# Expert outputs accumulated into stored rows, and every stage given a new place

## What is computed

```python
xn = layernorm(x)
x = x + cosformer(xn) + moe0(xn)      # linear attention, 16 heads; 2 shared experts + top 4 of 16
xn = layernorm(x)
x = x + softmax_attn(xn) + moe1(xn)   # causal, rotary, 16 heads of 8; one expert of 8 per token

# moe1, the last part: each token belongs to the expert with its greatest probability
route = softmax(xn @ router_w + router_b)
e, p = argmax(route), max(route)
a, g = split(xn @ w1[e])              # 128 -> 2 x 512
out = (silu(a) * g) @ w2[e] * p       # 512 -> 128, times that probability
```

## Time and profile before

| what | before |
|---|---|
| device time, median of 3 runs | 1369.88 us (1368.84 to 1372.6) |
| profiled execution: span, first to last instruction | 1371.5 us |
| profiled execution: own time | not given apart from the span; the 3 runs lie on both sides of it |
| PE busy | 1209.3 us, 88% of the span |
| DVE, ACT, POOL busy | 991.5, 912.8, 692.6 us |
| last matmul of the run starts | 1336.68 us |
| output DMAs | 4 of 1024 KB, 7.9 us to landing |
| granted TensorE clock, mean | 0.959 |

### The profile page before, as it was taken

How to read it: one execution, slowest core, us unless ns; L and a number is a source line. 1 busy time by engine, 2 the same in 40 slices (tenths; PEclk the granted TensorE clock), 3 DMA queues, 4 the chain that set the end, 5 groups by cost and what they waited for, 6 DMA issues and landing times.

```text
span 1371.5 us, 28942 instructions
## 1 busy us (share of the span) xinstructions
PE 1209.3 (88%) x10216; PEld 700.1 (51%) x10216; DVE 991.5 (72%) x2378; ACT 912.8 (67%) x1233; POOL 692.6 (50%) x1093
## 2 busy tenths in 40 slices
PE   2675999999999999999999999999986999899990
PEld 1342445445454545454454545454432476799990
DVE  2163888888888988888888989888868462344545
ACT  1141777778687868777786877787773667577760
POOL 6324455554536464554545464655543345466760
PEclk9898999999999999999999999999996799999995
DMA  7323505050524416060515335060615210111118
GB/s 224 63 57 64 111 19 115 20 103 27 96 53 71 91 32 120 11 115 20 103 34 88 72 52 105 19 120 14 111 37 171 74 29 25 31 48 50 50 48 250
DMA packets 80300, 100.90 MB, mean 74 GB/s; under 512 B 8800, under 2 KB 56672, under 8 KB 79776
## 3 DMA queue, kind: packets, MB, share of 16 engines
q1 hardware_dynamic: 75680, 89.85, 29.9%
q0 software_dynamic: 4480, 9.22, 2.3%
HBM read 73.50 MB, written 25.01 MB: 72 GB/s over the span
## 4 chain that ended last, share of the span: by engine, by line
PE 63%; DVE 20%; issue 5%; ACT 4%; POOL 4%; DMA 3%; ACTq 0%; SPq 0%; DVEq 0%; POOLq 0%
PE PS L628 9%; PE PS L595 8%; PE PS L440 7%; PE PS L484 7%; PE PS L561 5%; PE PS L639 4%; PE PS L580 4%; PE PS L423 4%; DVE xn L824 3%; PE PS L434 2%; DVE nm L985 2%; DMA early<-gate_rows 2%; PE PS L462 2%; PE PS L570 2%; DVE ra L933 1%
## 5 line engine op out<-in xcount | busy, mean ns | idle before, releaser
L735 ACT ACTIVATE flow<-PS 128x1024 f32<-128x1024 f32 x320 | 321.2, 1028 | 129.4 <-PE PS L580 112.1
L1146 POOL TENSOR_SCALAR_AFFINE_SELECT flow<-flow 128x256 f32<-128x256 f32 (+1 forms) x448 | 191.0, 444 | 374.3 <-ACT flow L735 371.7
L595 PE MATMUL PS<-flow 128*32 128x512 f32 (+3 forms) x2048 | 181.2, 455 | 6.2 <-POOL flow L1146 6.2
L985 DVE TENSOR_REDUCE nm<-PS 128x2 f32<-128x1024 f32 x128 | 154.6, 1220 | 42.3 <-PE PS L549 38.9
L1133 POOL TENSOR_TENSOR early<-early 128x512 f32<-128x512 f32 x128 | 160.7, 1270 | 20.9 <-DMA early<-gate_rows 20.0
L484 PE MATMUL PS<-early,down 128*128 128x512 f32 x288 | 151.8, 637 | 18.4 <-POOL early L1133 17.9
L726 ACT COPY qp<-PS 2x1024 f16<-2x1024 f16 x128 | 128.5, 1004 | 51.0 <-PE PS L570 49.8
L440 PE MATMUL PS<-xnT,up 128*128 128x512 f32 x288 | 152.6, 625 | 3.7 <-DVE at L908 3.4
L987 DVE TENSOR_REDUCE nm<-PS 128x2 f32<-128x768 f32 x128 | 121.6, 950 | 32.4 <-PE PS L549 32.3
L628 PE MATMUL PS<-xsT,w1s 128*128 128x128 f32 x1152 | 141.5, 276 | 3.0 <-DVE act L1079 2.9
L1076 DVE SCALAR_TENSOR_TENSOR tanh<-tanh,PS 128x512 f32<-128x512 f32 x72 | 49.5, 687 | 130.0 <-ACT tanh L769 130.0
(11 more groups left out here) (178 smaller groups left out, 2263.3 us busy)
## 6 DMA issues: line engine op xcount, KB each, us to landing
early<-gate_rows SPq DMA_DIRECT2D x32, 1024.0 KB, 10.8
qp<-relay_q SPq DMA_DIRECT2D x64, 128.0 KB
kp<-relay_k SPq DMA_DIRECT2D x64, 128.0 KB
xsb<-xs SPq DMA_DIRECT2D x76, 64.5 KB, 1.8
relay_k<-qkh SPq DMA_DIRECT2D x32, 128.0 KB, 2.3
early<-in_w SPq DMA_DIRECT2D x1, 4096.0 KB, 14.8
out_y<-X SPq DMA_DIRECT2D x4, 1024.0 KB, 7.9
relay_q<-qkh SPq DMA_DIRECT2D x16, 128.0 KB, 2.3
```

The costliest lines, as they stand in the source:

```text
L595: ins = pe.matmul(m.PS[32 * j:32 * j + 32, m.PV, kt * P:], m.vst[b % 2][:, kt, 4 * g + j, :], m.pt[:, r, k * L + o:k * L + o + L - kt * P] ...
L735: act.activation(m.pt[:, n % RING, :], m.PS[:, i:i + 2, :].rearrange("p k c -> p (k c)"), ACT.Exp, scale=1.0 / SCALE).then_inc(s["exp"], 1)
L985: dve.tensor_reduce(nm[:, 3, 2 * n:2 * n + 2], ps, AX_X, ALU.max, negate=True).then_inc(s["max"], 1)
L1146: ins = pool.affine_select(part, part, [[0, part.shape[1]], [1, P]], ALU.is_ge, nothing, base=0, channel_multiplier=-1)
```

## The change

Two things are changed together.

**The outputs of the second experts.** `ys` and its end are gone. `store` writes each batch's 512 rows of `X` to the output as soon as its attention is added (256 KB each, SP). ScalarE multiplies a tile's output by the token's probability while it copies it out of PSUM, and puts it into `X` itself, whose 64 tiles serve as the buffers. `scatter` (POOL) is an indirect DMA with `compute_op=ALU.add`: it adds the 128 rows onto the rows in the output tensor. The probability travels with the row in `xs`, whose rows are now 130 wide; blank rows carry a spare destination (2048 extra rows at the end of the output tensor, cut off afterwards) and probability 0, written from constants by 18 pad DMAs instead of 9. The destination is now one VectorE copy (`rows`) instead of three GpSimd operations. The first scatter waits for all 16 stores. `load` has 12 buffers and waits for the output copy of the tile 12 before it; the tile list has 72 entries instead of 76.

**The places.** All numbers of the tables are new, and each stage of each of the 72 tiles has its own number; from tile 31 on they are again 1.3 apart. 22 instead of 21 tiles use the shared banks.

```diff
 NTILE = B * NT + E1
 RING = 4
 SL = 5
-U = 4
-NTAB = NTILE + U
+U = 12
+NPAD = 2 * E1
+FIRSTS = B * NT - 2 * NT
+ROW = D + 2
+NTAB = NTILE
...
 FIRST = placed(
-    stats0=[-57.35],
-    norm0=[-49.85],
...
+    stats0=[-58.08],
+    norm0=[-51.44],
...
+    q=[-45.19],
+    kv=[-41.49],
...
 ATTENTION = placed(
-    score=[0, 0.1, 1.45, 3.05, 7.4, 8.2, 9.25, 10.3, 12.35, 13.05, 13.85, 14.05, 14.6, 14.7, 15.2, 15.35, 15.75,
...
-    mparts=[-2.85, 3.3, 8.15, 10.35],
-    mrows=[-0.85, 5.2, 10.4, 12.1],
...
+    max=[-9.06, -8.97, -8.72, -3.65, -2.28, -2.01, 0.93, 0.98, 1.36, 3.14, 4.03, 4.58, 4.76, 4.87, 5.22, 5.84, 6.37,
+         8.49, 10.01, 10.22],
+    mparts=[-2.14, 3.93, 5.97, 10.4],
+    mrows=[-0.98, 6.02, 10.06, 11.08],
...
+    out=[24.82],
+    store=[25.4])
...
 
     def outputs(_, n):
         act.wait_ge(s["yo_mm"], n + 1)
-        act.wait_ge(s[f"d_ys{n % U}"], 16 * (n // U + 1))
-        act.copy(m.ysb[:, n % U, :], wk(("outputs", 0, n))[:, 0:D]).then_inc(s["ycopy"], 1)
+        if n == 0:
+            act.wait_ge(s["d_out"], 16 * (B - 2))
+        if n == FIRSTS:
+            act.wait_ge(s["d_last"], 16 * 2)
+        if n == B * NT:
+            act.wait_ge(s["d_head"], 16 * E1)
+        act.activation(m.X[:, n % (B * NT), :], wk(("outputs", 0, n))[:, 0:D], ACT.Copy,
+                       scale=m.xsb[:, n % U, D + 1:D + 2]).then_inc(s["ycopy"], 1)
...
-        then(dve.tensor_reduce(m.pmax[:, b * NT:(b + 1) * NT], m.p1[:, :, :], AX_X, ALU.max))
+        then(dve.tensor_reduce(m.xn[1][:, :, D + 1], m.p1[:, :, :], AX_X, ALU.max))
...
+    def rows(_, n):
+        u = n % U
+        dve.wait_ge(s[f"d_xs{u}"], 16 * (n // U + 1))
+        dve.tensor_copy(m.rowu[:, n:n + 1], m.xsb[:, u, D:D + 1]).then_inc(s["rows"], 1)
...
-    n = B * NT // Q
-    for q in range(Q):
-        y, xq = m.yg[:, q * n:(q + 1) * n, :], m.X[:, q * n:(q + 1) * n, :]
-        dve.wait_ge(s[f"d_xs{q}"], 16 * (NTILE // U + 2))
-        then(dve.tensor_tensor(y, y, m.pmax[:, q * n:(q + 1) * n].unsqueeze(2).to_broadcast([P, n, D]), ALU.mult))
-        dve.tensor_tensor(xq, xq, y, ALU.add).then_inc(s["final"], 1)
```

```diff
-LAST = [(-19.5, "w1", 0), (-4.5, "w2", 0), (-13, "spares", 0)] + [(-12.4 + 1.2 * k, "tables", k) for k in range(6)]
...
+LAST = placed(
+    w1=[-27.19],
+    w2=[-11.16],
+    tables=[-14.1, -12.56, -10.07, -6.93, -6.76, -6.28],
+    pads=[-19.91],
...
+NBETWEEN = 22
```

```diff
-    def rows(_, n):
-        u = n % U
-        pool.wait_ge(s[f"d_xs{u}"], 16 * (n // U + 1))
-        pool.wait_ge(s[f"d_ys{u}"], 16 * (n // U + 1))
-        if n:
-            pool.wait_ge(s["nextspare"], n)
-        pool.tensor_scalar(m.isno[:, :], m.xsb[:, u, D:D + 1], 0.0, m.spare[:, 0:1], ALU.is_lt,
-                           ALU.mult).then_inc(s["spare"], 1)
-        pool.wait_ge(s["spare"], n + 2)
-        pool.tensor_scalar(m.rowu[:, u:u + 1], m.isno[:, :], m.xsb[:, u, D:D + 1], None, ALU.add).then_inc(s["rows"], 1)
-        pool.tensor_scalar(m.spare[:, :], m.spare[:, :], float(P), None, ALU.add).then_inc(s["nextspare"], 1)
-
-    def outputs(_, n):
-        u = n % U
+    def scatter(_, n):
+        if n == 0:
+            pool.wait_ge(s["d_out"], 16 * (B - 2))
+            pool.wait_ge(s["d_last"], 16 * 2)
+            pool.wait_ge(s["d_spare"], 16)
         pool.wait_ge(s["ycopy"], n + 1)
         pool.wait_ge(s["rows"], n + 1)
         alone()
-        pool.indirect_dma_start(m.ys_d, bass.IndirectOffsetOnAxis(ap=m.rowu[:, u:u + 1], axis=0),
-                                m.ysb[:, u, :], None).then_inc(s[f"d_ys{u}"], 16)
-
-    share = dict(stats0=stats0, stats1=stats1, q=q, gated=gated, score=scores, rope=rope, sort=sort, spares=spares, rows=rows,
-                 outputs=outputs)
+        pool.indirect_dma_start(m.rows_d, bass.IndirectOffsetOnAxis(ap=m.rowu[:, n:n + 1], axis=0),
+                                m.X[:, n % (B * NT), :], None,
+                                compute_op=ALU.add).then_inc(s["d_head" if n < E1 else "d_added"], 16)
...
         sp.wait_ge(s["rowzero"], 1)
+        marks = const(m, K_SP).rearrange("p (j c) -> p j c", c=2)
         for e in range(E1):
             row = sp.value_load(m.ti[0:1, 0, e:e + 1], min_val=0, max_val=E1 * CAP - P)
-            sp.dma_start(m.xs_d[bass.ds(row, P), :], m.zeros[:, :]).then_inc(s["d_pad"], 16)
-        sp.dma_start(m.xs_d[E1 * CAP:E1 * CAP + P, :], m.zeros[:, :]).then_inc(s["d_pad"], 16)
+            sp.dma_start(m.xs_d[bass.ds(row, P), 0:D], m.zeros[:, 0:D]).then_inc(s["d_pad"], 16)
+            sp.dma_start(m.xs_d[bass.ds(row, P), D:], marks[:, e, :]).then_inc(s["d_pad"], 16)
+        last = m.xs_d[E1 * CAP:E1 * CAP + E1 * P, :].rearrange("(j p) c -> p j c", p=P)
+        sp.dma_start(last[:, :, 0:D], m.zeros[:, 0:D].unsqueeze(1).to_broadcast([P, E1, D])).then_inc(s["d_pad"], 16)
+        sp.dma_start(last[:, :, D:], marks[:, E1:, :]).then_inc(s["d_pad"], 16)
...
             sp.wait_ge(s["rows"], n - U + 1)
-        row = sp.value_load(m.ji[0:1, 2, n:n + 1], min_val=0, max_val=E1 * CAP)
+            sp.wait_ge(s["ycopy"], n - U + 1)
+        row = sp.value_load(m.ji[0:1, 2, n:n + 1], min_val=0, max_val=E1 * CAP + (E1 - 1) * P)
         sp.dma_start(m.xsb[:, u, :], m.xs_d[bass.ds(row, P), :]).then_inc(s[f"d_xs{u}"], 16)
 
-    share = dict(gT=gT, parts=parts, relay=relayed, w1=w1, w2=w2, pads=pads, load=load)
+    def store(b, i):
+        if b == 0:
+            sp.dma_start(m.spare_d, m.zeros[:, 0:D].unsqueeze(1).to_broadcast([P, NPAD, D])).then_inc(s["d_spare"], 16)
+        sp.wait_ge(s["x2"], b + 1)
+        sp.dma_start(m.out_d[:, b], m.X[:, b * NT:(b + 1) * NT, :]).then_inc(s["d_out" if b < B - 2 else "d_last"], 16)
...
-    n = B * NT // Q
-    for u in range(U):
-        sp.wait_ge(s[f"d_ys{u}"], 16 * (NTILE // U + 1))
-    for q in range(Q):
-        src = m.ys_d[q * n * P:(q + 1) * n * P, :].rearrange("(t p) d -> p t d", p=P)
-        sp.dma_start(m.yg[:, q * n:(q + 1) * n, :], src).then_inc(s[f"d_xs{q}"], 16)
-    for q in range(Q):
-        sp.wait_ge(s["final"], q + 1)
-        sp.dma_start(m.out_d[:, q * B // Q:(q + 1) * B // Q].rearrange("p b t d -> p (b t) d"),
-                     m.X[:, q * n:(q + 1) * n, :]).then_inc(s["d_out"], 16)
-    sp.wait_ge(s["d_out"], 16 * Q)
+    sp.wait_ge(s["d_out"], 16 * (B - 2))
+    sp.wait_ge(s["d_last"], 16 * 2)
+    sp.wait_ge(s["d_spare"], 16)
+    sp.wait_ge(s["d_head"], 16 * E1)
+    sp.wait_ge(s["d_added"], 16 * (NTILE - E1))
```

More of the change, by code:

```diff
@@ L173 @@
-LAST += [(tile(n + 1) + 0.15, "outputs", n) for n in range(NTILE)]
-NBETWEEN = sum(tile(n) < max(at for at, *_ in ATTENTION) + 2 * STEP for n in range(NTILE))
+    stats0=[-58.08],
+    norm0=[-51.44],
+    xnT0=[-48.05],
+    kvr=[-47.08, -46.86, -45.57, -45.5],
+    up=[-42.62, -41.13, -39.39, -38.79, -37.95, -35.66, -35.52, -35.17, -34.42],
+    q=[-45.19],
+    kv=[-41.49],
+    route0=[-43.9],
+    gate=[-41.31],
+    attn0=[-40.41],
+    gT=[-40.1],
+    at0T=[-36.19])
+SECOND = placed(
+    down=[-34.37, -33.84, -33.19, -31.55, -30.58, -30.51, -29.84, -29.66, -28.77],
+    gated=[-36.88, -36.48, -36.24, -35.69, -33.62, -33.57, -32.72, -29.94],
+    x1=[-27.9],
+    stats1=[-27.11],
+    norm1=[-25.85],
+    xnT1=[-24.82],
+    rope=[-23.89, -22.79],
+    parts=[-23.55, -21.62],
+    relay=[-20],
+    v=[-18.51],
+    logits=[-23.88],
+    route1=[-20.64],
+    expert=[-20.3],
+    ranks=[-16.69],
+    sort=[-18.85, -17.19, -15.96, -14.65])
@@ L1083, in vector_program @@
                  stats1=stats1, xnT1=xnT1, logits=logits, rope=rope, parts=parts, route1=route1, expert=expert,
-                 ranks=ranks, max=maxima, mparts=mparts, heads=heads, out=out, tables=tables, hidden=hidden)
+                 ranks=ranks, max=maxima, mparts=mparts, heads=heads, out=out, tables=tables, rows=rows,
+                 hidden=hidden)
     dve.wait_ge(s["d_x"], 16)
```

110 lines of the change are left out of this document (35 added, 75 removed), and 28 rows, old and new, of tables (hidden, load, outputs, rows).

## The result

The changed kernel takes 1352.08 us (median of 4 runs, 1349.87 to 1355.94), the kernel before, on the same chip, 1369.36 us (4 runs). The ratio is 0.9876, 95% interval 0.9858 to 0.9893: faster by 1.2%, 17 us, where 52 were forecast. The profiled execution has a span of 1351.0 us, against 1371.5. That is 20.5 us less and not 17, since the profiled execution of the kernel before was the slowest of its four (1372.6 us).

What follows compares the result with a forecast made beforehand. PE was taken as the limit in the tiles, PE's waits in the even flow, a chain of waits at the end. Terms -29.3, -17.0, -2.1, -3.5 sum to -51.9: span 1319.6, median 1318.0 us; 8 in 10 within 1299 to 1344.

Steps and rivals of the forecast that it cites:

- The end: After the last tiles: read-back, eight VectorE instructions and last stores go, run ends when the last accumulating scatter lands; -29.3 us.
- rival 4: Output scatters: accumulating scatters don't overlap, so the kernel gets slower, 1422 us; decides from 1.99 us each; chance 0.05.
- The landing of 3.2 us: Last accumulating scatter: lands 3.2 us after issue, the middle between 2.2 us (plain scatter) and 4.2 us (read, then write).
- The start: First batch: `q` ahead of the first `up` and `route0` removes `attn0`'s wait for GpSimd's product; -2.1 us.
- The even flow: 200 to 1000 us: `norm0` before the last but one reduction removes PE's wait for `mt`, others halve; -17.0 us net.
- Rival 3: Even flow: `norm0` as long at its new place, last reduction late, 0.8 us stay per batch; 1328 us, chance 0.10.
- That `mt` was late by `norm0` alone: Even flow before the change: VectorE was 1.57 us late for the reduction before `mt`, by `norm0` alone.
- The middle: Last attention to the tiles: w1 and fourth table step moved, one more tile with a single bank pair; -3.5 us.
- w1's early place: Before the tiles: w1 loaded before the relays, so `tables` no longer waits for the last sort's scatters; -2.5 us.
- the table steps' 2.2 us: Last batch: fourth table step after the first three `max` instead of before, so PE gets them earlier; -2.2 us.
- Rival 5: Output scatters: they cost 2.0 to 2.7 us each or start late, moving the end; say 1345 us, chance 0.03.
- Rival 1: Whole kernel: the end goes, new places bring nothing as each removed wait returns as another; 1340.6 us, chance 0.17.
- Rival 2: Before the tiles: the clock no longer falls, and more of the waits go; 1299 us, chance 0.13.

## Why the prediction failed

- **The end, right.** -29.3 forecast, -28.5 measured behind the last mark; from the issue of the last scatter alone it is 32.5 before and 3.2 now, the forecast to 0.1 us. Two inputs were off, both to the bad side: a scatter takes 1.56 us and not 1.07, and they begin at 1206 and not at 1196. They did no harm only because there was slack: at 1.87 us apart they came close to the limit of 1.99 that rival 4 named. The landing of 3.2 us was the middle between two bounds, so its agreement is partly luck. By the Trainium skill, "DMA: Bandwidth & Descriptors", section "Latency and other measured facts", the estimate was 3.0 us, which this run does not tell from 3.2.
- **The start, right in its mechanism, its size not told from the variation.** -2.1 and -2.2. The first `attn0` no longer waits for GpSimd and starts at 35.05 instead of 36.74 us. But the first mark lies between 223.6 and 225.7 us in the seven kernels with these places and this `norm0`, and at 225.6 in the one with the old even flow and the new tiles.
- **The even flow, wrong, and the step that sank the forecast.** I wrote that "GpSimd multiplies and scatters all through this stretch, so the new place alone doesn't make `norm0` shorter", and left its 3.1 us as they were. GpSimd's mean load was the wrong thing to look at. At the new place GpSimd's products stand closer together, with fewer masks between, and `norm0` takes 7.1 to 8.2 us. PE then waits 2.4 us a batch for the reductions behind it, the sign of being wrong that the prediction named (a new wait of 1 us in each batch). That is 10 us more of idle PE in 12 batches. The other 15 us are a lower clock (0.98), for which the term had nothing. The wait for `mt` did go, as forecast. Whether the rest of the term was sound is not shown: -18.0 us came with `norm0` off VectorE, not with its 3.1 us at the new place, which no run has, so that this is near -17.0 may be luck. Rival 3 had the late reduction but priced it at 0.8 us a batch, since it took the old length for the length of all places. The rule of the Trainium skill, "SBUF — State Buffer", section "Who interferes with whom", cited against the term, was the one to follow; the runs agree that the two exclude each other, and show waits beyond the one instruction that it speaks of (4.94 us across three products and a mask). The sign was in the earlier trace rows: its longest instruction, 2.03 us, less its own 0.34, is more than GpSimd's product of 1.27 us, so one instruction can wait for more than one of GpSimd's.
- **That `mt` was late by `norm0` alone, half wrong.** Taking `norm0` away in the old order wins 0 to 5 us of 14.5, since the last step of `mt` meets GpSimd as well.
- **The middle, right in sign and mis-sized.** -3.5 forecast, -14.4 measured. The wait that w1's early place was to remove is gone, its 2.5 us are not settled, and of the table steps' 2.2 us no run shows a gain. The tiles' new places among the attention's, which I had counted only as +1.2 for one more tile with a single pair of banks, win some 11 us, and only together with the attention's new places. Which tile's step does it stays open.
- **The rivals.** Rival 5 (1345) was nearest in time, and by luck: the scatters, 1.87 us apart, did not hold the end up. Rival 1 (the places bring nothing, 1340.6) came next; its premise, waits that come back as others, fits `norm0` on ScalarE in the old order, which won nothing, but not in the new one. Rival 2's clock before the tiles did not come: it is 0.55 as before.

## What to carry to other kernels

Before moving a VectorE instruction of a form that shares with GpSimd, read GpSimd's timeline at both places, not its mean load, and look which instructions it has there: it worked without a pause at the old place too, where `norm0` took 3.1 us and not 7.6. Where no free place serves both GpSimd and the one who waits for the result, change the engine; here that was worth 45 us, more than any move of `norm0` (20 us at most). Two tables of places that were made for each other should be exchanged together: from batch 12 to the last each half exchange (221 and 218 us) was slower than both whole pairs (205 and 190).
